# Key/value stage: normalised keys turned by VectorE in 32 by 32 blocks and stored by four transfers, in a cross-attention and routed FFN kernel

## What is computed

```
h = layernorm(x)
q = (h @ Wq + bq)              # 16 heads of 128
k = (ctx @ Wk + bk)            # 4 key heads of 128
v = (ctx @ Wv + bv)
q = rmsnorm(q) * qn_w          # per head of 128
k = rmsnorm(k) * kn_w
scores = q . k / sqrt(128)     # each key head serves 4 query heads
x = x + softmax(scores) @ v @ Wo
x = x + routed_ffn(layernorm(x))
```

## Time and profile before

| what | value |
|---|---|
| runs (three), us | 832.25, 836.52, 835.98; median 835.98 |
| profiled execution, us | 833.15 |
| its span, first to last instruction, us | 831.4 |
| TensorE busy | 787.2 us (95%) |
| VectorE busy | 566.4 us (68%) |
| ScalarE busy | 470.7 us (57%) |
| GpSimd busy | 548.3 us (66%) |
| mean granted TensorE clock | 0.983 of full speed |

### The profile page before, as it was taken

The page is one execution under the profiler, slowest core; times in us unless marked ns, Lnnn a source line. Parts: engine busy times, 40 slices in busy tenths (PEclk is TensorE's granted clock), DMA queues, the critical chain, the costliest instruction groups (busy, mean ns, idle before and its releaser), DMA issues. The chain is left out here.

```text
span 831.4 us, 14178 instructions
## 1 busy us (share of the span) xinstructions
PE 787.2 (95%) x3968; PEld 654.6 (79%) x3968; DVE 566.4 (68%) x1049; ACT 470.7 (57%) x1618; POOL 548.3 (66%) x611
## 2 busy tenths in 40 slices
PE   6999996999999999999999999999987799989997
PEld 4888874888888888888888888888865577877886
DVE  4545455687787787787787787778777688754122
ACT  4555455575675675675665665665654256554440
POOL 2333355677777777776776876876867297756980
PEclk9999997999999999999999999999999899999999
DMA  7666663222322332332332332332254655213620
GB/s 231 200 212 205 200 218 97 60 82 68 103 83 68 102 90 64 101 91 67 95 95 63 96 94 63 98 91 63 76 158 155 231 186 182 103 54 125 204 99 25
DMA packets 85001, 97.66 MB, mean 117 GB/s; under 512 B 8112, under 2 KB 48176, under 8 KB 84976
## 3 DMA queue, kind: packets, MB, share of 16 engines
q1 hardware_dynamic: 84400, 95.52, 37.6%
q0 software_dynamic: 576, 1.84, 0.6%
HBM read 63.77 MB, written 17.30 MB: 98 GB/s over the span
## 5 line engine op out<-in xcount | busy, mean ns | idle before, releaser
L900 POOL TENSOR_TENSOR wp_lo<-raw,wp_hi 128x512 fp32r<-128x512 f32 x88 | 113.9, 1336 | 34.8 <-ACT wp_hi L970 34.8
L1080 ACT ACTIVATE p_row<-s_row,neg_max 128x128 f32<-128x128 f32 x256 | 100.0, 395 | 63.8 <-DVE neg_max L1374 63.7
L824 POOL TENSOR_TENSOR p_row<-p_row,p_inv 128x512 f32<-128x512 f32 x64 | 66.8, 1044 | 98.1 <-DVE p_inv L1389 98.1
L1794 PE MATMUL b_y<-wo_hi,oT_hi 128*128 128x512 f32 x256 | 107.5, 420 | 3.4 <-DVE oT_lo L1278 3.4
L1796 PE MATMUL b_y<-wo_hi,oT_lo 128*128 128x512 f32 x256 | 101.8, 398 | 0.0
L1795 PE MATMUL b_y<-wo_lo,oT_hi 128*128 128x512 f32 x256 | 101.8, 398 | 0.0
L1794 PE MATMUL b_q<-wq_hi,xT_hi 128*128 128x512 f32 x248 | 97.8, 394 | 0.0
L1796 PE MATMUL b_q<-wq_hi,xT_lo 128*128 128x512 f32 x248 | 97.4, 393 | 0.0
L1795 PE MATMUL b_q<-wq_lo,xT_hi 128*128 128x512 f32 x248 | 97.3, 392 | 0.0
L970 ACT ACTIVATE oT_hi<-b_o 128x512 fp32r<-128x512 f32 x64 | 38.4, 599 | 102.2 <-PE b_o L1796 100.3
L856 POOL TENSOR_TENSOR pT_lo<-raw,pT_hi 128x512 fp32r<-128x512 f32 x62 | 81.0, 1307 | 0.9 <-ACT pT_hi L970 0.9
(11 more groups left out here) (369 smaller groups left out, 2206.3 us busy)
## 6 DMA issues: line engine op xcount, KB each, us to landing
raw<-raw SPq DMA_DIRECT2D x248, 64.0 KB, 2.1
cx<-in_ctx_dram SPq DMA_DIRECT2D x16, 256.0 KB, 2.7
raw<-in_L_xattn_Wq_dram SPq DMA_DIRECT2D x16, 256.0 KB, 2.7
raw<-in_L_xattn_Wo_dram SPq DMA_DIRECT2D x16, 256.0 KB, 3.2
v_store<-v_out SPq DMA_DIRECT2D x16, 256.0 KB, 3.3
k_store<-k_out SPq DMA_DIRECT2D x16, 256.0 KB, 2.0
xr<-in_x_dram SPq DMA_DIRECT2D x16, 256.0 KB, 3.1
v_raw<-v_store SPq DMA_DIRECT2D x16, 256.0 KB, 3.0
```

What stands on the lines that cost most here:

```text
L824: pool.tensor_tensor(p_row[:], p_row[:], per_head(p_inv, S), ALU.mult).then_inc(p_normed, 1)
L900: last = pool.tensor_tensor(wp_lo[n % NSLOT][:, c, :], raw[RAW_OF[n]][:, c, :], wp_hi[n % NSLOT][:, c, :].bitcast(fp32), ALU.subtract)
L1080: e = act.activation(place, row, ACT.Exp, bias=neg_max[:, h:h + 1], accum_out=p_sum[:, h:h + 1])
L1794: pe.matmul(dst, left[0], right[0], start=start, stop=False)
```

## The change

TensorE no longer turns the keys, and ScalarE no longer copies them out of PSUM. VectorE turns `k_row` in blocks of 32 by 32 into `k_tr`, whose partitions hold four groups (token blocks i) of 32 head places. Four transfers, one for each group of partitions, put the blocks into place in `k_store`: each writes, into the 128 rows of the batch, one piece of 128 columns. A row of `k_store` is now ordered by token block, head, token within the block, and `k_high` and `k_low` read it through a view that sets it right. The key weight and the score scale are multiplied into `qw` (`qw_scaled`), with which the queries are scaled anyway. `k_stored` now counts 64 a batch instead of 16.

```diff
+            k_tr = sb_in(st, "k_tr", [P, 4, NKV, 32])
...
+        def stored_keys(tile_):
+            return tile_.rearrange("p (i g s) -> p i g s", i=4, g=NKV)
+        def keys_by_part(part):
+            return kT[:, :, part, :].rearrange("p g (i s) -> p i g s", i=4)
...
             def store_k(b):
-                sp.wait_ge(k_weighted, b + 1)
-                sp.dma_start(k_store[bass.ds(b * P, P), :], k_out[:]).then_inc(k_stored, 16)
+                sp.wait_ge(k_turned, b + 1)
+                for i in range(4):
+                    rows_ = k_store[b * P:(b + 1) * P, i * P:(i + 1) * P]
+                    sp.dma_start(rows_.rearrange("(j d) x -> d j x", j=4),
+                                 k_tr[32 * i:32 * i + 32].rearrange("d j g s -> d j (g s)")
+                                 ).then_inc(k_stored, 16)
...
-                pool.tensor_tensor(kT[:, :, 1, :], src.rearrange("p (g s) -> p g s", g=NKV),
-                                   kT[:, :, 0, :].bitcast(fp32), ALU.subtract).then_inc(kT_lo_done, 1)
+                pool.tensor_tensor(keys_by_part(1), stored_keys(src), keys_by_part(0).bitcast(fp32),
+                                   ALU.subtract).then_inc(kT_lo_done, 1)
...
-            def weigh_k(b, bank=b_kT):
-                act.wait_ge(k_turned, b + 1)
-                wait(act, k_stored, 16 * b)
-                act.activation(k_out[:], bank[:], ACT.Copy, scale=kw[:, 0:1]).then_inc(k_weighted, 1)
...
-                copy(kT[:, :, 0, :], src.rearrange("p (g s) -> p g s", g=NKV)).then_inc(kT_hi_done, 1)
+                copy(keys_by_part(0), stored_keys(src)).then_inc(kT_hi_done, 1)
...
-            dve.tensor_scalar(kw[:], kw[:], 1.0 / SCALE, None, ALU.mult).then_inc(kw_scaled, 1)
+            dve.tensor_scalar(qw[:], qw[:], kw[:, 0:1], 1.0 / SCALE, ALU.mult, ALU.mult).then_inc(qw_scaled, 1)
...
+            def k_turn(b):
+                dve.wait_ge(k_normed, b + 1)
+                wait(dve, k_stored, 64 * b)
+                dve.transpose(k_tr[:], k_row[:].rearrange("p g (j d) -> p j g d", j=4)).then_inc(k_turned, 1)
...
-            def kv_batch(b, par):
+            def kv_batch(b, par, first=False):
                 turn_c(b + 1, 1 - par)
+                if not first:
+                    k_turn(b - 1)
                 key_rows(b)
...
             turn_c(NB - 1, 1)
+            k_turn(NB - 3)
             key_rows(NB - 2)
...
+            k_turn(NB - 2)
             key_rows(NB - 1)
+            dve.wait_ge(qw_scaled, 1)
...
             value_rows(NB - 1)
+            k_turn(NB - 1)
             weights_over(dve)
...
-            def turn_k(b, bank=b_kT):
-                pe.wait_ge(k_normed, b + 1)
-                wait(pe, k_weighted, b)
-                turn(bank, k_row[:].rearrange("p h d -> p (h d)")).then_inc(k_turned, 1)
...
-                if not first:
-                    turn_k(b - 1)
...
-            turn_k(NB - 1, b_pT)
```

More of the change, by code:

```diff
@@ L202, in xattn_then_routed_ffn @@
             k_row = sb_in(st, "k_row", [P, NKV, HD])
-            k_out = sb_in(st, "k_out", [P, NKV * S])
+            k_tr = sb_in(st, "k_tr", [P, 4, NKV, 32])
             v_out = sb_in(st, "v_out", [P, NKV * HD])
@@ L310, in xattn_then_routed_ffn @@
         b_rank = b_xT
-        b_c, b_k, b_v, b_kT = b_xT, b_q, b_s, b_qT
+        b_c, b_k, b_v = b_xT, b_q, b_s
         f_proj = [b_q, b_y]
@@ L328, in xattn_then_routed_ffn @@
         const_loaded = sem("const_loaded")
-        kw_scaled = sem("kw_scaled")
+        qw_scaled = sem("qw_scaled")
         wk_loaded = [sem(f"wk_loaded{i}") for i in range(2)]
@@ L348, in xattn_then_routed_ffn @@
         k_turned = sem("k_turned")
-        k_weighted = sem("k_weighted")
         k_stored = sem("k_stored")
@@ L546, in keys_over @@
         def keys_over(eng):
-            eng.wait_ge(k_stored, 16 * NB)
+            eng.wait_ge(k_stored, 64 * NB)
             eng.wait_ge(v_stored, 16 * NB)
@@ L619, in _ @@
             spread(bq_row[:, 0:W], bq[0:W]).then_inc(first_bias_loaded, 16)
-            sp.wait_ge(k_stored, 16 * (NB - 2))
+            sp.wait_ge(k_stored, 64 * (NB - 2))
             load_first_k()
@@ L985, in _ @@
             act.wait_ge(const_loaded, 48)
-            act.wait_ge(kw_scaled, 1)
-            def weigh_k(b, bank=b_kT):
-                act.wait_ge(k_turned, b + 1)
-                wait(act, k_stored, 16 * b)
-                act.activation(k_out[:], bank[:], ACT.Copy, scale=kw[:, 0:1]).then_inc(k_weighted, 1)
+            act.wait_ge(qw_scaled, 1)
             def squares(t):
@@ L1014, in kv_batch @@
                 sq.then_inc(k_squared, 1)
-                if not first:
-                    weigh_k(b - 1)
                 if last:
@@ L1082, in exps @@
                 e.then_inc(p_exped, 1)
-            weigh_k(NB - 1, b_pT)
             weights_over(act)
@@ L1320, in kv_batch @@
                 weights_low(b, par)
-            kv_batch(0, 0)
+            kv_batch(0, 0, True)
             with dve.Fori(0, NB // 2 - 2) as g:
```

## The result

| what | before | after |
|---|---|---|
| median of 8 runs each, us | 834.19 (831.65 to 837.84) | 840.01 (838.97 to 842.05) |
| ratio after to before, 95% interval | | 1.0071 [1.0046, 1.0097] |
| profiled execution, its span, us | 833.15, 831.4 | 839.49, 837.8 |
| TensorE busy, mean granted clock | 787.2 us, 0.983 | 784.5 us, 0.983 |
| VectorE busy | 566.4 us | 582.9 us |

The kernel is slower by about 0.7%, 5.8 us of medians; the forecast was 841 us, about +6. Read the new profile in the order in which the old one was read.

What follows compares the result with a forecast made beforehand. TensorE bounds the key/value stage at 6.40 us a batch; the key-row loop at 6.89 would take over. +0.41, +4.9 and +0.73 sum to +6.0 us on about 834.6: 841 us, the forecast's own range 837 to 844.

Steps and rivals of the forecast that it cites:

- the trap: Key/value stage: VectorE stands still while GpSimd normalises the keys; a held `wq_lo` subtraction takes 1.56 us instead of 0.68.
- the key-row loop: VectorE and GpSimd, from one normalisation's end to the next: 6.89 us with the transpose, over TensorE's 6.04.
- The lap: Time from one batch's key rows to the next batch's in the key/value stage; forecast 6.89 us, from 6.40.
- The step from the transpose to the key rows: VectorE: key rows wait for the block transpose just ahead, starting 0.73 us after it; lower end 0.60.
- The count of laps: Key/value stage: second lap +0.41 us, then ten more laps at 0.49 each, +4.9 us.
- the sum: Whole kernel: +0.41 for the second lap, +4.9 for ten more, +0.73 ahead of batch 14's key rows; +6.0 us.
- TensorE's price of a key turn: TensorE, key/value stage: each batch's key turn costs 0.36 us; 16 turns give 5.8 us at most.
- The transfers: Rival, much slower: four small transfers delay the value store, transfer loop 7.48 us, 846 to 849 us; chance 0.12.
- The alternating laps: Rival, nothing to measure: GpSimd and `wq_lo` alternate in going first, mean lap 6.3 to 6.6 us, 833 to 836; chance 0.20.
- the 0.21 us of margin: Key/value stage: GpSimd's normalisation starts at 5.85 us, ahead of `wq_lo` at 6.06, counted from the last normalisation's end.
- two rivals: The faster case, chance 0.10, and the nothing-to-measure case of alternating laps, chance 0.20.
- the faster case: Rival: weight subtractions get ahead of the normalisation, laps 6.20 or 6.04 us, 827 to 832 us; chance 0.10.

## Why the prediction was right

**The bound and the trap.** TensorE's 6.40 gave way to the key-row loop, closed by GpSimd's lock on `wq_lo`, as forecast. The lap came out at 6.96 where 6.89 was worked out, `wq_lo` at 1.2 to 1.6 us in ten of twelve laps (0.68 and 0.87 in the others) where 1.3 to 1.5 in each was given. The lock was shown from both sides: without GpSimd's normalisation the loss is gone though the transpose stays, and a transpose that has nothing to do with the keys brings it back.

**The step from the transpose to the key rows** was mis-sized: 0.80 us (61.69 to 62.49 in one lap, 68.66 to 69.46 in the next), where 0.73 was taken and 0.60 was the lower end. The experiment with a transpose that nobody waits for gives the other price in the same place: 69.01 to 69.63, 0.62; in the changed kernel the query rows behind the last transpose, which do not wait for it, start 0.63 after it (127.37 to 128.00). So the wait of an instruction for the one ahead on the same engine costs 0.18 us here, about 2 us over eleven laps. The section of the Trainium skill named in the prediction (VectorE: DVE Perf Modes, The DRAIN you can't avoid) has this semaphore cost nothing; the trace does not agree, at 0.80 against 0.62.

**The count of laps** was one short. From the third batch to batch 13 there are eleven laps, not the ten of the sum; the missing one is 0.5 us. Ahead of batch 14's key rows the transpose took 0.81 (111.95 to 112.76), for 0.73, but the delay grew by 0.62 only (6.46 to 7.08): in that lap the wait for the value store ends last, and it ended 0.19 sooner after the key rows (108.75 - 104.28 = 4.47; 102.48 - 97.82 = 4.66 before). With the measured sizes the sum is 0.49 + 11 x 0.56 + 0.62 = 7.3, and the first query turn came 7.2 later, at 127.55 where 126.4 was forecast. Two things that the sum does not have partly cancel in this: the first lap grew by 0.21 (5.49 to 5.70; the sum put it at nothing), and the profiled execution of after reached its first key rows 0.37 sooner (15.08, before 15.45). That start lies anywhere from 15.06 to 16.98 in the nine profiled executions, in kernels with the change and without it.

**The total** then came out at +6.3 on the profiled executions, against +6.0: the sizes were too small by about 1.2 together, and the landing of the first probabilities, 1.05 us late in the profiled execution of before, made up for nearly all of it. The near hit of the total is therefore partly luck; the 5.8 us between the medians agree with it within the interval of the ratio (3.8 to 8.1 us of 834.19).

**Taken as nothing and right:** the four transfers, shown by the kernel with one; the issue time on SyncE's queue; the strided view of the keys in the attention stage (1285 ns, not the 1307 that the probabilities had suggested); ScalarE's saved copies; VectorE's extra work as such, shown by the transpose behind the key rows. For the issue time and ScalarE's saved copies no run of their own was made.

**TensorE's price of a key turn** was set at 0.36 us, its own work without it at 6.04. It is 6.40 - 5.93 = 0.47: the first product behind a turn also takes longer (65.47 to its successor at 65.78 in the trace before, 0.31, where products further on follow one another by 0.23), which is 0.08 of the 0.11 that the forecast lacked. Nothing hung on it here, since TensorE was no longer the bound, but the gain that lay behind the loops was larger than thought. Its idle time, forecast as about 0.8 us a batch, shows as 0.57 (5.75 over 70.40 / 6.96 laps), though 6.96 - 5.93 = 1.03 is not needed. The ends of products are modelled in the profile, so a part may not show as idle; that is not tested.

**The rivals.** The transfers fell by experiment. The alternating laps did not come: one lap of the stretch flipped its order,

```profile
52.08 0.68 DVE L1278 TENSOR_TENSOR wq_lo<-raw,wq_hi 128x512 f32 x1
52.08 1.58 POOL L803 TENSOR_TENSOR k_row<-k_row,k_rs 128x512 f32<-128x512 f32 x1
52.68 1.53 DVE L1278 TENSOR_TENSOR wo_lo<-raw,wo_hi 128x512 f32 x1
```

and gained 0.06 us by it (key rows at 48.63 and 55.53, 6.90 apart). There `wq_lo` and the normalisation began together, GpSimd waited and then held `wo_lo`, and the end of the hold was nearly the same. What counts is how much of VectorE's work is through when GpSimd's product runs. In the kernel with one transfer `wq_lo` was nearly through once:

```profile
23.77 0.68 DVE L1275 TENSOR_TENSOR wq_lo<-raw,wq_hi 128x512 f32 x1
24.34 1.04 POOL L800 TENSOR_TENSOR k_row<-k_row,k_rs 128x512 f32<-128x512 f32 x1
24.37 1.56 DVE L1275 TENSOR_TENSOR wo_lo<-raw,wo_hi 128x512 f32 x1
```

That lap took 6.36 (key rows at 20.89 and 27.25), one subtraction of 0.60 less than 6.96, and in the next GpSimd was first again. So the 0.21 us of margin, on which the prediction hung two rivals, mattered less than it says: a flip by so little gives back 0.06, a whole subtraction ahead of the normalisation gives 0.6 in its lap, and both subtractions ahead, lap after lap, took the earlier value store. That the faster case was a real one, at 5.9 us a lap, is shown by that experiment. Laps that alternate do occur in the kernel before with the earlier store, where `wq_lo` takes 0.68 and 1.56 in turn, under TensorE's 6.40.

## What to carry to other kernels

Before work is moved off the busiest engine, list the other loops that lie close under its period and see which of them the moved work enters: here an engine idle for half of its time had no room on the one stretch that closes a loop with a neighbour's lock, and the same 0.70 us cost 4.1 us ahead of the key rows and nothing behind them. If a change loses for such a reason, look for what holds the loop rather than drop the change: an issue order on a queue (a store that stood behind loads which wait for later work) turned +5.8 us into -9.2 (each against its own runs of the kernel before). Close the account of a predicted total by intermediate points of the trace (a row at the end of each stage), since errors of one us in different terms can cancel.

## What was not expected of the hardware

- A VectorE instruction that waits for the block transpose just ahead starts 0.80 us after it, one that waits for nothing 0.62: the wait on its own engine's last instruction is not free.
- The hold between VectorE and GpSimd goes both ways, and taking turns doesn't end it: GpSimd's product took 1.04 us when it was first, 1.46 when `wo_lo` had begun 0.13 us ahead of it, and 1.58 when it came with `wq_lo`, after which `wo_lo` took 1.53 in its turn.
- Not every GpSimd instruction holds VectorE: with the earlier value store `wq_lo` took 0.68 or 0.69 us in each steady lap beside GpSimd's 128 by 4 root (59.79 beside 59.43 to 60.44), where beside the 128 by 512 product it took up to 1.55 in the changed kernel.
- The value store landed in 3.3 us at the median in the changed kernel, right behind two weight loads, and in 2.5 when issued ahead of them, 1.1 us behind the context load (58.81 to 59.90). In the kernel before the same move left it at 3.1; there it follows 0.5 us behind the context load (57.04 to 57.56). What sets the landing is not shown.
